# A delta rule whose loop over couples is written out, and a mixture of experts that reads each tile's expert number once

## The reference, cut to what matters

```python
x = x + L0_attn(xn) + L0_ffn(xn)      # gated delta rule; mixture of experts
x = x + L1_attn(xn) + L1_ffn(xn)      # linear attention; nested softmax attention

def step(S, inp):                      # gated delta rule, 16 heads of 64
    q_t, k_t, v_t, g_t, b_t = inp
    Sk = einsum('bhkv,bhk->bhv', S, k_t)
    delta = einsum('bhv,bhk->bhkv', v_t, k_t) - einsum('bhv,bhk->bhkv', Sk, k_t)
    S = exp(g_t)[..., None, None] * S + b_t[..., None, None] * delta
    o_t = einsum('bhkv,bhk->bhv', S, q_t)

topk_scores, topk_idx = top_k(logits + router_bias, 2)      # of 16 experts
hidden = silu(gate_all) * up_all
out = einsum('nk,nkd->nd', combine, einsum('nke,ked->nkd', hidden, down_proj))
```

## Time and profile before

| | |
|---|---|
| runs before | 4819.50, 4818.39, 4813.27 us; median 4818.39 us |
| the profiled execution | 4783.38 us, with a span of 4781.6 us |
| PE busy | 4446.1 us, 93% of the span |
| VectorE, ScalarE, GpSimd busy | 69%, 40%, 22% |
| granted TensorE clock, mean | 0.972 |

### The profile page before, as it was taken

One profiled execution on the slowest core, in us unless ns is written; L12 is line 12 of the kernel. 1 busy time (PEld: TensorE's weight loads), 2 busy tenths in 40 slices (PEclk: granted clock), 3 DMA queues, 4 the chain that ended last, 5 costly groups with the idle time before them and its releaser, 6 DMA issues. The chain is left out here.

```text
span 4781.6 us, 154458 instructions
## 1 busy us (share of the span) xinstructions
PE 4446.1 (93%) x64527; PEld 2868.5 (60%) x64527; DVE 3305.4 (69%) x5496; ACT 1912.6 (40%) x2685; POOL 1037.3 (22%) x1042
## 2 busy tenths in 40 slices
PE   5999699999999999999987879999999999999998
PEld 3444499889889888987655634444444444444443
DVE  5899755555555555554338977878787878787877
ACT  2888311111111111111233426656565656565654
POOL 1000143344334333432007760000000000000000
PEclk9999899999999999999998969999999999999999
DMA  3544411111111111111233440000000000000000
GB/s 121 169 129 126 135 50 53 54 46 51 52 54 50 53 53 47 50 53 58 74 120 105 111 106 9 9 13 9 13 9 13 9 13 9 13 9 13 9 13 9
DMA packets 261647, 250.25 MB, mean 52 GB/s; under 512 B 51712, under 2 KB 230016, under 8 KB 260256
## 3 DMA queue, kind: packets, MB, share of 16 engines
q1 hardware_dynamic: 240528, 209.39, 14.6%
q0 software_dynamic: 6144, 16.79, 1.1%
q10 hardware_dynamic: 14352, 14.55, 0.9%
HBM read 135.27 MB, written 105.38 MB: 50 GB/s over the span
## 5 line engine op out<-in xcount | busy, mean ns | idle before, releaser
L2201 DVE TENSOR_REDUCE part_max<-p_m 128x1 f32<-128x512 f32 x2118 | 1363.2, 685 | 380.8 <-PE p_m L2043 373.3
L2183 ACT ACTIVATE prob<-p_s 128x1024 f32<-128x1024 f32 x1024 | 1047.6, 1023 | 751.0 <-PE p_s L2107 748.9
L2062 PE MATMUL p_o<-prob,v_one 128*64 128x512 f32 x4096 | 1055.1, 593 | 5.2 <-ACT prob L2183 1.8
L2043 PE MATMUL p_m<-keys,queries 96*64 96x512 f16 x4236 | 661.4, 387 | 28.0 <-DMA keys<-parts_d 20.4
L2107 PE MATMUL p_s<-queries,keys 97*64 97x512 f16 x4096 | 618.9, 380 | 0.0
L2107 PEld LDWEIGHTS p_s<-queries,keys 97*64 97x64 f16 x4096 | 228.1, 109 | 599.3 <-issue 593.8
L2043 PEld LDWEIGHTS p_m<-keys,queries 96*64 96x64 f16 x4236 | 238.6, 108 | 311.2 <-DVE part_max L2201 56.4
L2011 POOL TENSOR_TENSOR attn<-o_num,o_inv 32x512 f32<-32x512 f32 x64 | 81.0, 1266 | 1459.5 <-DVE o_inv L2220 1453.1
L833 PE MATMUL pd_pre<-inv,step 64*64 64x64 f32 x10240 | 374.4, 219 | 17.9 <-issue 15.4
L2062 PEld LDWEIGHTS p_o<-prob,v_one 128*64 128x64 f32 x4096 | 287.5, 136 | 164.3 <-issue 15.8
L833 PEld LDWEIGHTS pd_pre<-inv,step 64*64 64x64 f32 x10240 | 342.7, 135 | 46.0 <-issue 45.7
(11 more groups left out here) (245 smaller groups left out, 6701.5 us busy)
## 6 DMA issues: line engine op xcount, KB each, us to landing
q_d<-conv_q SPq DMA_DIRECT2D x16, 1024.0 KB, 5.1
v_d<-conv_v SPq DMA_DIRECT2D x16, 1024.0 KB, 5.1
k_d<-conv_k SPq DMA_DIRECT2D x16, 1024.0 KB, 6.5
sums<-sums_d SPq DMA_DIRECT2D x128, 128.0 KB, 2.9
k_t<-k_d SPq DMA_DIRECT2D x32, 512.0 KB, 4.6
q_t<-q_d SPq DMA_DIRECT2D x32, 512.0 KB, 3.4
v_t<-v_d SPq DMA_DIRECT2D x32, 512.0 KB, 3.3
slots_d<-zero ACTq DMA_DIRECT2D x1, 10112.0 KB, 31.2
```

What stands on the lines that cost most here:

```text
L2043: last = te.matmul(p_m[k % 2][x * HALF:(x + 1) * HALF, :], queries[0:ROW, p, hh, at:at + HALF], keys[0:ROW, 2 * p + hh, kb * BLK:(kb + 1) ...
L2062: product = te.matmul(p_o[64 * hh:64 * hh + VW, :], g.v_one[:, j, p, hh:hh + 2, :].rearrange("p a d -> p (a d)"), prob[:, j % 2, hh, :], s ...
L2183: a.activation(prob[:, j % 2], p_s[j % 2][:], ACT.Exp, scale=SCORE_SCALE).then_inc(exp_d, 1)
L2201: v.tensor_reduce(part_max[:, hh * SUB + sub, kb:kb + 1], p_m[k % 2][:], AX.X, ALU.max).then_inc(red_d, 1)
```

## The change

In `phase_delta` the loop goes: all 33 calls of `one` are written out with fixed numbers, on every engine, and `TRIPS` falls away. A new helper `wait_each` waits for each semaphore with the value as a constant in the instruction, without a register and without the wait for the constants; it replaces `wait_apart` in every wait of PE in this phase and in GpSimd's `scatter`. In `phase_experts` the number of a tile's expert is read once, in the step in which the tile is transposed, behind that step's `gate_up` matmuls; the register is kept for `gate_up` a step later and for `down` three steps later.

```diff
+def wait_each(eng, *waits):
+
+    for sem, value in waits:
         eng.wait_ge(sem, value)
...
-    TRIPS = (LAST - 3) // 2
...
     def couples(engine, one):
-        for it in (-1, 0):
-            one(fixed(engine, it), fixed(engine, it + 1), fixed(engine, it + 2))
-        with looped(nc, engine, TRIPS) as i:
-            mid = Couple(engine, i * 2 + 2, 0, i + 2)
-            late = Couple(engine, i * 2 + 3, 1, i + 2)
-            one(Couple(engine, i * 2 + 1, 1, i + 1), mid, late)
-            one(mid, late, Couple(engine, i * 2 + 4, 0, i + 3))
-        for it in range(2 * TRIPS + 1, LAST + 1):
+        for it in range(-1, LAST + 1):
             one(fixed(engine, it), fixed(engine, it + 1), fixed(engine, it + 2))
...
         def half(n, x, k):
             freed = (rows_d[x], n.now) if k == 1 else (up_d[x], n.level[k - 1])
-            wait_apart(pe, g, freed, (lowc_d[x], n.level[k]))
+            wait_each(pe, freed, (lowc_d[x], n.level[k]))
             each(p_pre[x], of(upper[x]), of(low_1[x] if k == 1 else inv_low[x])).then_inc(half_d[x], 1)
...
-            wait_apart(pool, g, (place_d, n.now), (rows_in[n.odd], n.filled))
+            wait_each(pool, (place_d, n.now), (rows_in[n.odd], n.filled))
...
+        expert = {}
+
+        def find_expert(j):
+            expert[j] = pe.value_load(g.owner[0:1, j:j + 1], min_val=0, max_val=NE - 1)
+
         def one(x, gu, h, dn):
...
             if gu is not None:
-                e = pe.value_load(g.owner[0:1, gu:gu + 1], min_val=0, max_val=NE - 1)
                 pe.wait_ge(sglu_d, 2 * NB)
...
-                    last = te.matmul(..., gate_up[:, c, bass.ds(e, 1), :]...)
+                    last = te.matmul(..., gate_up[:, c, bass.ds(expert[gu], 1), :]...)
                 last.then_inc(gu_d, 1)
+            if x is not None:
+                find_expert(x)
             if h is not None:
...
             if dn is not None:
-                e = pe.value_load(g.owner[0:1, dn:dn + 1], min_val=0, max_val=NE - 1)
                 pe.wait_ge(sadd_d, 2 * NB)
...
-                te.matmul(..., down[:, bass.ds(e, 1), :]...)
+                te.matmul(..., down[:, bass.ds(expert.pop(dn), 1), :]...)
```

More of the change, by code:

```diff
@@ L123, in wait_apart @@
     for (sem, _), value in zip(waits, values):
+        eng.wait_ge(sem, value)
+def wait_each(eng, *waits):
+    for sem, value in waits:
         eng.wait_ge(sem, value)
@@ L848, in keys_keys @@
             r = n.ring[x]
-            wait_apart(pe, g, (k_in[n.odd], n.key_loads), (up_d[x], n.level[0]))
+            wait_each(pe, (k_in[n.odd], n.key_loads), (up_d[x], n.level[0]))
             each(p_pre[x], of_couple(k_t, r), of_couple(k_t, r)).then_inc(kk_d[x], 1)
@@ L853, in keys_queries @@
             r = n.ring[x]
-            wait_apart(pe, g, (q_in[n.odd], n.filled))
+            wait_each(pe, (q_in[n.odd], n.filled))
             each(p_low[x], of_couple(k_t, r), of_couple(q_t, r)).then_inc(qk_d[x], 1)
         def key_rows(n, x):
-            wait_apart(pe, g, (upper_d[x], n.now))
+            wait_each(pe, (upper_d[x], n.now))
             each(p_pre[x], of_couple(k_t, n.ring[x]), eye).then_inc(row_d[x], 1)
@@ L867, in low @@
             if k == 1:
-                wait_apart(pe, g, (inv1_d[x], n.now), (step_d[x], n.level[k]))
+                wait_each(pe, (inv1_d[x], n.now), (step_d[x], n.level[k]))
             else:
-                wait_apart(pe, g, (step_d[x], n.level[k]))
+                wait_each(pe, (step_d[x], n.level[k]))
             for p, hs in heads():
@@ L882, in residual @@
             r = n.ring[x]
-            wait_apart(pe, g, (v_in[n.odd], n.filled), (kg_d[x], n.now), (ocp_d, n.begun[x]), (state_d, n.ended[x]))
+            wait_each(pe, (v_in[n.odd], n.filled), (kg_d[x], n.now), (ocp_d, n.begun[x]), (state_d, n.ended[x]))
             for p, hs in heads():
@@ L889, in updates @@
         def updates(n, x):
-            wait_apart(pe, g, (tok_d, n.last), (up_d[x], n.level[NL]), (ress_d, n.ended[x]))
+            wait_each(pe, (tok_d, n.last), (up_d[x], n.level[NL]), (ress_d, n.ended[x]))
             each(p_b, of(inv_fin, n.ring[x]), of(resid)).then_inc(w_d, 1)
@@ L894, in outputs @@
             r = n.ring[x]
-            wait_apart(pe, g, (qg_d[x], n.now), (att_d[x], n.now), (u_d, n.ended[x]))
+            wait_each(pe, (qg_d[x], n.now), (att_d[x], n.now), (u_d, n.ended[x]))
             for p, hs in heads():
@@ L901, in new_state @@
         def new_state(n, x):
-            wait_apart(pe, g, (rows_d[x], n.now), (udec_d, n.ended[x]))
+            wait_each(pe, (rows_d[x], n.now), (udec_d, n.ended[x]))
             each(p_b, of(k_row, n.ring[x]), of(u_dec)).then_inc(new_d, 1)
@@ L907, in project @@
             if pairs[0] == 0:
-                wait_apart(pe, g, (wo_in, 16), (state_d, n.stated[1]), (ocp_d, n.ended[1]))
+                wait_each(pe, (wo_in, 16), (state_d, n.stated[1]), (ocp_d, n.ended[1]))
             for p in pairs:
@@ L1319, in one @@
                 for c in range(KC):
-                    last = te.matmul(p_gu[gu % 2][:, 0:2 * HID], x_t[:, gu % 2, c, :], gate_up[:, c, bass.ds(e, 1), :].rearrange("p a n -> p (a n)"),
+                    last = te.matmul(p_gu[gu % 2][:, 0:2 * HID], x_t[:, gu % 2, c, :], gate_up[:, c, bass.ds(expert[gu], 1), :].rearrange("p a n -> p (a n)"),
                                      start=c == 0, stop=c == KC - 1)
                 last.then_inc(gu_d, 1)
+            if x is not None:
+                find_expert(x)
             if h is not None:
@@ L1333, in one @@
                 pe.wait_ge(htc_d, dn + 1)
-                te.matmul(p_y[dn % 2][:, 0:D], hid_t[:, dn % 2, :], down[:, bass.ds(e, 1), :].rearrange("p a n -> p (a n)"),
+                te.matmul(p_y[dn % 2][:, 0:D], hid_t[:, dn % 2, :], down[:, bass.ds(expert.pop(dn), 1), :].rearrange("p a n -> p (a n)"),
                           start=True, stop=True).then_inc(dn_d, 1)
```

## The result

The changed kernel takes 4664.94 us (median of 4 runs, 4662.89 to 4669.35) against 4815.83 us (4811.53 to 4819.5) for the kernel before on the same chip: 151 us less, a ratio of 0.9693 with a 95% interval of 0.9678 to 0.9707. Its profiled execution took 4664.79 us, its span is 4663.0 us.

What follows compares the result with a forecast made beforehand. Prediction: PE's stream of small matmuls bounds the delta stage. Jumps 83.8, loop ends 4.1 and moves 3, less 3 for fetching, give 88 us; with experts' 35, 123 us off 4818.4 makes 4695, range 4650 to 4740.

Steps and rivals of the forecast that it cites:

- free crossings: Delta stage, rival: fetching runs far enough ahead that 28 us of small idle spots go too; 4667 us, chance 0.05.
- The case that was forecast: Whole kernel: delta stage gains 88 us and experts 35, giving 4695 us; chance 0.69.
- The jumps, 83.8 us: Delta loop: 13 taken jumps cost PE idle time, then slow matmuls, 6.4 us each; writing out removes them.
- What writing out adds to PE, and the waits: Delta stage: writing out adds little fetching for PE; dropped second waits and moves cost nothing.
- The ends of the loop and the moves in couples 0 and 29: First and late pipeline passes: loop set-up and exit stalls give 4.1 us, register moves 3 (0 to 6.2).
- The other engines' fetching: Delta stage: code of VectorE, ScalarE, GpSimd and SyncE is now fetched, costing 3 us (0 to 18).
- The experts, 35: Experts stage: one read fewer makes PE the bound, steps 1.70 instead of 2.16 us; gain 35 us (15 to 39).
- Dearer written-out couples: Delta stage, rival: straight code makes pipeline passes 52.2 us; stage gains 4, experts 39, time 4779; chance 0.10.
- Experts keep their pace: Experts stage, rival: the remaining read stalls PE as two did, or an `x_tile` load is late; 4730 us, chance 0.11.
- Slower by fetching: Delta stage, rival: five engines fetching take turns, pipeline passes run 55.6 us; 4881 us, chance 0.05.
- issue before L833 near 28 us: Delta stage, sign of being right: PE's unexplained idle time before L833 products falls from 85.7 to near 28 us.
- The base: Whole kernel: gain reckoned on the profiled execution (4783.4 us), applied to the 4818.4 median, 35 us higher.

Runs made afterwards that it cites:

- e1: The kernel before, unchanged, run once more for a second profile: 4815.4 us.
- e5: The kernel before with its delta loop cut from 14 trips to 7 and steps 15 to 28 written out: 4772.3 us, ratio 0.9916.
- e6: The kernel before with the hint for the loop's backward edge left out: 4819.77 us, ratio 1.0019.
- e3: The kernel before with the delta loop written out and `wait_each` in that stage, both expert reads kept: 4701.47 us, ratio 0.9771.
- e2: The kernel before with only the delta loop written out, `wait_apart` and both expert reads kept: 4759.99 us, ratio 0.9895.
- e9: The changed kernel with the always-met constants wait put back before its delta-stage waits, without register moves: 4672.13 us, ratio 0.9716.
- e4: The kernel before with only the experts' part of the change: 4771.51 us, ratio 0.992.
- e11: The changed kernel with a second expert read, for `down`, in the same place as the first: 4702.67 us, ratio 0.9772.
- e10: The changed kernel with its one expert read put right behind the transposes, ahead of the `gate_up` products: 4685.23 us, ratio 0.9736.
- e7: The changed kernel with one indirect DMA per couple instead of two, second experts' rows not written: 4619.22 us, ratio 0.9601.
- e8: The changed kernel with the row loads and both indirect DMAs moved from the delta to the projection stage, on GpSimd: 4608.99 us, ratio 0.958.

## Why the prediction came out as it did

The prediction had 123 us of gain, to 4695; it was 151, to 4664.9. That is inside the range, but only because the range was widened for the free crossings: the forecast's own bounds gave 4682 at best. Their 97 us for the delta stage were added up wrongly, too (83.8 + 4.1 + 6.2 is 94; the 3 was counted beside the 6.2 that holds it), and 109.5 were measured. The case that was forecast is the one that happened, and none of its terms of gain was too large.

- **The jumps, 83.8 us.** Measured 13 x 6.6 = 86 us (e1), and e5 confirms that the cost goes with their number. The reading was right: a branch of 3.7 us, then matmuls at the lower clock (0.53). That the time is a late target is borne out by e6, where the branch is 1 us dearer without the hint.
- **What writing out adds to PE, and the waits: the step that failed.** The prediction had "I cost these at nothing" for the dropped second wait and the moves, because POOL and ScalarE have room. It looked for cover on the wrong engines: of PE it only counted the moves that it makes today. It missed that `wait_apart` with constants would have made 2144 of them in straight code. That is 58.5 us, the difference of e3 and e2. The forecast survived because the change replaces the helper together with the loop, so the cost never appears in the sum. Against the loop, the written-out couples gain (50.07 - 49.73) x 27 = 9 us; the dropped extra waits explain about 7 of it by e9, with the overlap said there. Predicted: 0.
- **The ends of the loop and the moves in couples 0 and 29, 4.1 + 3.** Couples 0, 29 and 30 sum to 157.4 us in e1 and 145.6 in e3: 11.8. Less the 4.1 of the loop's ends that is 7.7, where the prediction had 3 and at most 6.2; "I give half to the moves" was too little. Three couples with the 60 to 70 moves each of e2, at 29 ns, are about 5.5 us; they were countable. e2 splits the 11.8 directly: its three couples sum to 151.8, so the loop's ends are 5.6 and the waits 6.2. And e6 shows the cause of the stall at the loop's exit to be the hint; "with no loop there is no exit" gave the right sum for another reason.
- **The other engines' fetching, -3.** Not seen. Couples in e3 are no dearer than plain ones before, although the second instruction queue carries 107 blocks instead of 83. The sum of the four: 86 + 9 + 12 + 0 = 107, against 109.5 measured by e3; the stage also began 2.3 us earlier in e3 than in e1, for which no part of the edit is a cause.
- **The experts, 35.** Measured 39.5 (e4), at the upper bound of 39. The 0.05 us added "as matmuls still have to wait for one another's copies" wasn't there: the median step is 1.65, exactly PE's own work. The reckoning of the sequencer, 0.96 + 2 x 0.6 = 2.16, gave e11 before it ran (2.17). It is no independent sum, as the 0.96 had been got from the old step of 2.16; what e11 adds is that the place of the second read doesn't matter. The 0.32 us for a lost cover were close for e10 (about 0.3 by the steps, and 20 us of time where 25 were expected).
- **The rivals.** Dearer written-out couples: false for the change, true for e2 (51.33 against 50.07), though by moves and not by straight code as such. Experts keep their pace: false. Slower by fetching: false; the longest couple takes 51.47 us. Free block crossings: in part true, and its 4667 us lies nearer the measured time than the forecast's 4695. The prediction counted 28 us of small idle spots; without jumps and without pauses 10.2 are left in e7. The sign "issue before L833 near 28 us" was met (30.5) by luck: in the changed kernel's trace 22.9 us of PE's idle time, at 63 spots, stand beside the indirect DMAs, where the profile of before had none. Whether the small spots shrank because nothing jumps any more or because the sequencer has fewer waits to work through was not told apart, so they and the 9 us above may in part be the same time. The Trainium skill's "Runtime: NRT & Kernel Launch" (Instruction fetch mechanics) calls the crossing mostly hidden, and e7's row agrees with it better than the 28 did.
- **The base.** The sum was made against the profiled execution, 35 us below the median of before, and carried over to the median unchanged, for which it gave no reason. It was right by luck: the pauses that go with this difference are in both kernels, and no row of the prediction could show them. Who compares the two profiled executions (4783.4 and 4664.8) finds a gain of 119 and takes the predicted 123 for nearly exact; it is 151 less the pauses that one of the two lacks.

## What to carry to other kernels

Before a loop is written out, count what its registers did: a helper that moves each wait value into a register is nearly free where the loop keeps them, and with its extra waits cost 58 us when 2144 moves of 29 ns stood ahead of small matmuls. Where PE's matmuls are as small as these (64 x 64), treat PE's sequencer as an engine with a budget of its own: sum its moves, extra semaphore waits (51 ns) and reads (0.6 us) per step before calling PE the bound. And profile the kernel before more than once; one execution of it lacked 32 us that all others had.

## What the runs showed of the hardware that was not expected

- Two indirect DMAs of GpSimd, 1.3 us apart, go with two pauses of 0.59 us in PE's stream of 64 x 64 products, which begin 0.2 and 0.9 us after the second one's start. One DMA instead of two: none. Both in a stage of products of 512 columns (e8): no time lost, and no such gap in the timelines read. What joins them (PE's instruction fetch, writes to memory, the profile's own records) is open; moving them was worth 56 us. Why one execution of the kernel before had no pauses is open, too.
- PE's taken jump back over two couples took 3.76 us with the hint and 4.79 without (medians), and 6.6 us in all with the matmuls at a granted clock of 0.53 behind it. The hint has a price, too: with it PE stalled 2.6 to 2.9 us behind the loop's last trip, without it not at all, and of the 18 us by which 13 jumps were shorter with it about 9 were left in the kernel's time.
- 545 semaphore instructions of 51 ns cost about a quarter of their duration (7 of 28 us, a difference near the noise), while the moves of 29 ns with the register waits behind them cost about 51 us, where the moves' duration is 62. Duration on the sequencer's row is not the price. What decides it was not traced.
